# Unsplit multiplication of every pair in the message sweep, from twelve load buffers

## The reference

```python
h = relu(layernorm(x))
msg = adj.T @ h                          # message sweep
x = x + msg * (1 / adj.sum(axis=0))[:, None]    # an infinite inverse becomes 0
h = relu(layernorm(x))
x1 = swish((adj @ h) @ W + b)            # second sweep, first half
x2 = swish((adj @ x1) @ W + b)           # second sweep, second half
x = x + x2
```

## Time and profile before

| | us |
|---|---|
| runs | 684.11, 687.60, 690.33 |
| median | 687.6 |
| profiled execution | 688.42 |
| its span | 686.6 |
| TensorE busy | 634.4 (92%) |
| GpSimd busy | 571.2 (83%) |
| VectorE busy | 523.1 (76%) |
| ScalarE busy | 301.4 (44%) |

### The profile page before, as it was taken

One profiled execution on the slowest core, in us unless ns is written; L12 is line 12 of the kernel. 1 busy time (PEld: TensorE's weight loads), 2 busy tenths in 40 slices (PEclk: granted clock), 3 DMA queues, 4 the chain that ended last, 5 costly groups with the idle time before them and its releaser, 6 DMA issues.

```text
span 686.6 us, 6755 instructions
## 1 busy us (share of the span) xinstructions
PE 634.4 (92%) x2212; PEld 404.0 (59%) x2212; DVE 523.1 (76%) x516; ACT 301.4 (44%) x378; POOL 571.2 (83%) x287
## 2 busy tenths in 40 slices
PE   4888978999998988899999999999999999799994
PEld 2355545666665645556666666667666557466553
DVE  3965789979978839777787777878778778577871
ACT  1943243264272343646445445445444434245250
POOL 2288488689788857998999999999999789599693
PEclk9989999999999998999999999999999999899998
DMA  8999996989999899999999999919999999999941
GB/s 277 352 303 306 298 366 246 329 300 333 329 292 309 286 233 250 345 345 317 328 345 330 329 345 317 279 25 195 327 345 345 315 328 332 305 252 347 311 94 31
DMA packets 155762, 199.80 MB, mean 291 GB/s; under 512 B 5456, under 2 KB 138832, under 8 KB 155728
## 3 DMA queue, kind: packets, MB, share of 16 engines
q1 hardware_dynamic: 86672, 133.18, 62.5%
q10 hardware_dynamic: 69056, 66.20, 35.0%
HBM read 197.26 MB, written 2.10 MB: 290 GB/s over the span
## 4 chain that ended last, share of the span: by engine, by line
PE 55%; POOL 20%; issue 12%; DMA 4%; ACT 3%; DVE 3%; ACTq 1%; SPq 1%; POOLq 0%
PE dg L351 20%; POOL a_lo L701 11%; PE dg L368 9%; PE dg L357 9%; PE dg L358 9%; POOL at_lo L715 7%; PE m_ps L277 4%; DMA raw<-in_adj_dram 2%; PE m_ps L376 2%; DMA h<-in_x_dram 2%; POOL norm L684 1%; PE m_ps L295 1%; PE m_ps L282 1%; PE m_ps L283 1%; ACTq L217 1%
## 5 line engine op out<-in xcount | busy, mean ns | idle before, releaser
L715 POOL TENSOR_TENSOR at_lo<-turned,at_hi 128x1024 fp32r<-128x1024 f32 x160 | 379.8, 2414 | 33.1 <-ACT at_hi L455 28.3
L602 DVE STREAM_TRANSPOSE turned<-raw 128x1024 f32<-128x1024 f32 x256 | 304.1, 1224 | 95.7 <-PE dg L351 41.9
L455 ACT ACTIVATE at_hi<-turned 128x1024 fp32r<-128x1024 f32 x160 | 167.3, 1057 | 208.8 <-DVE turned L602 122.2
L701 POOL TENSOR_TENSOR a_lo<-raw,a_hi 128x1024 fp32r<-128x1024 f32 x66 | 155.1, 2387 | 46.7 <-ACT a_hi L425 44.7
L351 PE MATMUL dg<-turned,f_w 128*128 128x512 f32 x384 | 182.4, 597 | 1.3 <-issue 1.3
L559 DVE TENSOR_TENSOR dg<-raw,dg 128x2048 f32<-128x2048 f32 x60 | 137.5, 2291 | 35.5 <-DMA raw<-in_adj_dram 33.6
L357 PE MATMUL dg<-at_hi,f_hi 128*128 128x512 f32 x320 | 134.9, 422 | 11.5 <-ACT at_hi L455 11.5
L368 PE MATMUL dg<-at_lo,f_hi 128*128 128x512 f32 x320 | 130.9, 490 | 3.1 <-POOL at_lo L715 3.1
L358 PE MATMUL dg<-at_hi,f_lo 128*128 128x512 f32 x320 | 128.4, 401 | 0.0
L277 PE MATMUL m_ps<-raw,h 128*128 128x512 f32 x248 | 116.6, 617 | 11.1 <-DMA raw<-in_adj_dram 11.1
L351 PEld LDWEIGHTS dg<-turned,f_w 128*128 128x128 f32 x384 | 73.2, 191 | 57.0 <-issue 48.5
(11 more groups left out here) (47 smaller groups left out, 258.8 us busy)
## 6 DMA issues: line engine op xcount, KB each, us to landing
raw<-in_adj_dram SPq DMA_DIRECT2D x64, 1024.0 KB, 8.9
raw<-in_adj_dram ACTq DMA_DIRECT2D x122, 512.0 KB, 13.5
raw<-in_adj_dram SPq DMA_DIRECT2D x118, 512.0 KB, 11.7
x<-in_x_dram SPq DMA_DIRECT2D x16, 128.0 KB, 13.5
out_dram<-zs ACTq DMA_DIRECT2D x16, 128.0 KB, 10.9
h<-in_x_dram SPq DMA_DIRECT2D x1, 768.0 KB, 9.3
h<-in_x_dram SPq DMA_DIRECT2D x1, 256.0 KB, 3.3
w<-in_L_gnn_W_dram ACTq DMA_DIRECT2D x1, 64.0 KB, 3.0
```

The costliest lines, as they stand in the source:

```text
L455: act.activation(at_hi[:, s % RING3], turned[:, unit % TURN], ACT.Copy).then_inc(hi3_done, 1)
L602: dve.transpose(dst, src).then_inc(t3_done, 1)
L701: pool.tensor_tensor(a_lo[:, s % RING1], raw1[:, v % RAW1, i], a_hi[:, s % RING1].bitcast(f32), ALU.subtract).then_inc(lo1_done, 1)
L715: pool.tensor_tensor(at_lo[:, s % RING3], turned[:, unit % TURN], at_hi[:, s % RING3].bitcast(f32), ALU.subtract).then_inc(lo3_done, 1)
```

## The change

All 64 pairs are multiplied whole. The rings `a_hi` and `a_lo`, the features `h_hi` and `h_lo`, and everything that fills or awaits them are gone; `raw1` has 12 buffers. A pair's load waits for pair v - 12, added and multiplied. The places in memory of the second sweep are ordered anew: `nT`, `zs` and `at_hi` lie over `raw1` buffers 0 to 3, pieces 1, 2 and 3 over buffers 4 to 9, so that their loads wait for pairs 54, 56 and 58. ScalarE issues its part of pieces 0 to 3 at the head of the last quarter, ahead of `relu2(2)` and the last `copy_message`. The second part of a message's turn moves from behind pair 6 to behind pair 9 of the next quarter, VectorE's add of it from 11 to 12 and its statistics from 12 to 13. GpSimd's scale and remainders of a quarter follow one another with nothing between.

```diff
-RAW1 = 5
-RING1 = 5
+RAW1 = 12
...
-        a_hi = sb("a_hi", [P, RING1, QC], f32r, into=sweep1)
-        a_lo = sb("a_lo", [P, RING1, QC], f32r, into=sweep1)
         h = sb("h", [P, NT, P], into=sweep1)
-        h_hi = sb("h_hi", [P, 2 * len(SPLIT_ROWS), P], f32r, into=sweep1)
-        h_lo = sb("h_lo", [P, 2 * len(SPLIT_ROWS), P], f32r, into=sweep1)
...
+        nT = sb("nT", [P, 2, QC], into=sweep2)
+        zs = sb("zs", [P, 2, QT, P], into=sweep2)
+        at_hi = sb("at_hi", [P, RING3, UC, GROUP], f32r, into=sweep2)
+        spare = sb("spare", [P, 1024], into=sweep2)
         raw3 = {n: sb(f"raw3_{n}", [P, GB, BC], into=sweep2) for n in (1, 2, 3)}
+        at_lo = sb("at_lo", [P, RING3, UC, GROUP], f32r, into=sweep2)
...
             if i in (1, 2, 3):
-                pairs = QUARTERS * PAIRS - (2 if i == 1 else 0)
-                eng.wait_ge(main1_done, pairs)
-                eng.wait_ge(lo1_done, 2 * split_before(pairs))
+
+                pairs = QUARTERS * PAIRS - RAW1 + 2 * i
+                eng.wait_ge(p1_done, pairs)
                 eng.wait_ge(deg_added, pairs)
...
                     sp.wait_ge(deg_added, back + 1)
-                    if whole1(back):
-                        sp.wait_ge(main1_done, back + 1)
-                    else:
-                        sp.wait_ge(lo1_done, 2 * split1(back) + 2)
+                    sp.wait_ge(p1_done, back + 1)
...
+            def p1(v):
                 q, k = v // PAIRS, v % PAIRS
+                pe.wait_ge(raw1_loaded[v % RAW1], 16 * (v // RAW1 + 1))
+                pe.wait_ge(h_ready, 2 * k + 2)
+                for half in range(2):
+                    cols = slice(half * 512, (half + 1) * 512)
+                    if k == 0 and q > 0:
+                        pe.wait_ge(msgT_copied, 2 * (q - 1) + half + 1)
+                    for i in range(2):
+                        mm = pe.matmul(m_ps[:, cols], h[:, 2 * k + i], raw1[:, v % RAW1, i, cols],
+                                       start=k == 0 and i == 0, stop=k == PAIRS - 1 and i == 1)
+                    if half == 0 and k == PAIRS - 1:
+                        mm.then_inc(half_done, 1)
+                mm.then_inc(p1_done, 1)
...
-                if v >= PAIRS and v % PAIRS == 6:
+                if v >= PAIRS and v % PAIRS == 9:
                     turn_message(v // PAIRS - 1, 1)
...
-            for v in splits1:
...
-            relu2(QUARTERS - 2)
-            load3(act, 1, ACT_BLOCKS)
-            copy_message(QUARTERS - 1)
+            for q in range(QUARTERS):
+                if q >= 2:
+                    relu2(q - 2)
+                if q == QUARTERS - 1:
                     load3(act, 0, SP_BLOCKS + ACT_BLOCKS)
+                    for i in range(1, RAW3):
+                        load3(act, i, ACT_BLOCKS)
+                    relu2(q - 1)
+                copy_message(q)
...
-                    if k == 11:
+                    if k == 12:
                         add_message(q, 1)
-                    if k == 12:
+                    if k == 13:
                         node_statistics(q, 1)
...
-            for v in splits1:
...
-            lo_h2(QUARTERS - 2)
+            for q in range(QUARTERS - 1):
+                scale_shift(q * QT, (q + 1) * QT, len(HEAD) + q)
+                lo_h2(q)
```

More of the change, by code:

```diff
@@ L98, in build @@
         f3_w = sb("f3_w", [P, UC * len(WHOLE3), P], into=sweep2)
[L99 to L103, removed]
+        gap = sb("gap", [P, 1536], into=sweep2)
         raw3[0] = sb("raw3_0", [P, GB, BC], into=sweep2)
@@ L145, in build @@
         block = ctx.enter_context(nc.Block())
[L149 to L159, removed]
         def whole3(unit):
@@ L260, in _ @@
         def _(pe):
-            def main1(v, half):
+            def p1(v):
                 q, k = v // PAIRS, v % PAIRS
[L264 to L314, removed]
+                pe.wait_ge(raw1_loaded[v % RAW1], 16 * (v // RAW1 + 1))
@@ L381, in _ @@
             for v in range(QUARTERS * PAIRS):
-                pair1(v)
+                p1(v)
                 if v >= PAIRS and v % PAIRS == 2:
                     turn_message(v // PAIRS - 1, 0)
-                if v >= PAIRS and v % PAIRS == 6:
+                if v >= PAIRS and v % PAIRS == 9:
                     turn_message(v // PAIRS - 1, 1)
@@ L413, in head @@
                 for t in range(*HEAD[b]):
-                    if t // 2 in SPLIT_ROWS:
-                        relu(h_hi[:, 2 * SPLIT_ROWS.index(t // 2) + t % 2], h[:, t], t)
                     relu(h[:, t], h[:, t], t).then_inc(h_ready, 1)
[L418 to L425, removed]
             def copy_message(q):
@@ L449, in hi3 @@
                 if s == 0:
-                    act.wait_ge(main1_done, QUARTERS * PAIRS)
-                    act.wait_ge(rest1_done, len(splits1))
+                    act.wait_ge(p1_done, QUARTERS * PAIRS)
+                    act.wait_ge(deg_added, QUARTERS * PAIRS)
                 if s >= RING3:
@@ L486, in _ @@
                 head(b)
-            for v in splits1:
-                if v >= PAIRS and v == splits1[split_before(v // PAIRS * PAIRS)]:
-                    copy_message(v // PAIRS - 1)
-                hi1(v)
-                if v >= 2 * PAIRS and v == splits1[split_before(v // PAIRS * PAIRS)]:
-                    relu2(v // PAIRS - 2)
-                if v // PAIRS == QUARTERS - 1 and v % PAIRS == 6:
+            for q in range(QUARTERS):
+                if q >= 2:
+                    relu2(q - 2)
+                if q == QUARTERS - 1:
                     load3(act, 0, SP_BLOCKS + ACT_BLOCKS)
-            relu2(QUARTERS - 2)
-            load3(act, 1, ACT_BLOCKS)
-            copy_message(QUARTERS - 1)
+                    for i in range(1, RAW3):
+                        load3(act, i, ACT_BLOCKS)
+                    relu2(q - 1)
+                copy_message(q)
             for unit in range(UNITS3):
@@ L502, in _ @@
                 i = unit // QU + RAW3 - 1
-                if unit in (1, 2):
-                    load3(act, unit + 1, ACT_BLOCKS)
                 if unit % QU == 0 and RAW3 <= i < len(PIECES) and i not in KEPT:
@@ L687, in scale_shift @@
                     .then_inc(norm_ready, 1)
-            def lo_h(k):
-                r = 2 * SPLIT_ROWS.index(k)
-                pool.wait_ge(h_ready, 2 * k + 2)
-                pool.tensor_tensor(h_lo[:, r:r + 2], h[:, 2 * k:2 * k + 2], h_hi[:, r:r + 2].bitcast(f32),
-                                   ALU.subtract).then_inc(h_lo_ready, 1)
-            def lo1(v):
-                for i in range(2):
-                    s = 2 * split1(v) + i
-                    pool.wait_ge(hi1_done, s + 1)
-                    if s >= RING1:
-                        pool.wait_ge(rest1_done, (s - RING1) // 2 + 1)
-                    pool.tensor_tensor(a_lo[:, s % RING1], raw1[:, v % RAW1, i], a_hi[:, s % RING1].bitcast(f32),
-                                       ALU.subtract).then_inc(lo1_done, 1)
             def lo_h2(q):
@@ L728, in _ @@
                 scale_shift(lo, hi, b)
-            for v in splits1:
-                q, k = v // PAIRS, v % PAIRS
-                if q == 0:
-                    lo_h(k)
-                if v == splits1[len(SPLIT_ROWS) - 3]:
-                    for late in SPLIT_ROWS[6:]:
-                        lo_h(late)
-                lo1(v)
-                if q >= 1 and k == 14:
-                    scale_shift((q - 1) * QT, q * QT, len(HEAD) + q - 1)
-                if q >= 2 and k == 3:
-                    lo_h2(q - 2)
-            lo_h2(QUARTERS - 2)
+            for q in range(QUARTERS - 1):
+                scale_shift(q * QT, (q + 1) * QT, len(HEAD) + q)
+                lo_h2(q)
             for unit in range(UNITS3):
```

9 lines of the change are left out of this document (2 added, 7 removed).

## The result

The changed kernel takes 683.4 us (median of 20 runs, 679.66 to 688.97), the kernel before 688.0 (median of 20, 682.87 to 697.07). The ratio is 0.994, with a 95% interval of 0.9911 to 0.9969. So it is faster, by 0.6% or some 4 us; the forecast was 679.3 us, 1.2%. The profiled execution has a span of 682.2 us, 4.4 less than before.

What follows compares the result with a forecast made beforehand. TensorE bounds the second sweep's middle; the message sweep is held by loads and late-released buffers. Span 686.6 - 8.3 (turn) = 678.3, plus 1.8 around it 680.1, less 0.8 for the median: 679.3 us; range 671 to 689.

Steps and rivals of the forecast that it cites:

- the 678.3 of the sum: Whole kernel: forecast span, 686.6 us before less 8.3 us saved in the turn between the sweeps.
- I let it start pair 20 at 86.5: Message sweep: TensorE starts pair 20 at 86.5 us, as 26.35 MB at 307 GB/s land at about 86 us.
- 151.4 + 5.4 + 0.7 = 157.5: Message sweep after pair 20: 44 pairs at 3.44 us, message turns 5.4 us, pipe refilling 0.7 us; end at 244.0.
- The 0.7 us of margin: Message sweep: 0.7 us added for the pipe refilling at the waits of the message turns.
- Rival (a): Message sweep ends at 248, not 244, through waits at quarter ends or the late copy; time 684 us; chance 0.25.
- rival (c): Message sweep: 512 B rows run at line rate, TensorE its own bound from 19.82, end 240.6, time 676 us; chance 0.05.
- The prices: TensorE's work: whole pair 3.44 us, split pair 2.73, so unsplit 0.71 dearer; 33 pairs add 23.4 us.
- Rival (b): Message sweep: loads behind pair 20 run at 307 GB/s, not 380; TensorE ends at 264, time 699 us; chance 0.13.
- The turn: Between the sweeps: GpSimd's fourteenth remainder ends at 283.7 against 292.05 us, through early pieces and relu; 8.3 us saved.
- VectorE's slip: Turn between the sweeps: VectorE has about 18 us of work against GpSimd's 14.3, so 1.1 us is allowed.
- Sweep 2 beyond: Second sweep behind the turn: only memory places change, cost 0 (-2 to +2 us); the 4.40 us stall may recur.
- The order of the queues: Last quarter: ScalarE's relus and load issues finish 5 us or more before the message copy; cost 0, otherwise 3 to 5.

## Why the prediction was right or wrong

**Wrong in size, in the main by one term.** The direction and the mechanism held: work added to TensorE, waits taken away, and the gain in the turn. The span came out 3.9 us over the 678.3 of the sum: 3.2 in the message sweep (247.2 for 244.0), 0.6 less in the turn, and 1.3 more behind it. The term that failed is "I let it start pair 20 at 86.5". TensorE started it at 87.04 + 3.44 = 90.5 us, 4.0 us later. I took the time at which the bytes had been moved (26.35 MB at 307 GB/s) for the time at which TensorE is fed. At 304 GB/s these bytes were moved by 87 us, but pair 20 was not there; the bytes of later loads are among them. VectorE's add of pair 20, which waits for the same load:

```profile
89.12 2.30 DVE L479 TENSOR_TENSOR dg<-raw,dg 128x2048 f32<-128x2048 f32 x1 [1.71 <-DMA raw<-in_adj_dram]
```

Two things were left out. The loads came 4.0 us apart in this stretch, not 3.8, and pair 18 began at 81.33; at 4.0 us a pair, pair 20 would have begun at 89.3 (it landed at 89.1), which is 2.8 of the 4.0. And the first message turn, 2.2 us behind pair 18, falls into a stretch without slack, of which 1.2 us came through; I had counted only the turns behind pair 20. All other terms of the sweep held: 156.7 us from pair 20 to the end against 151.4 + 5.4 + 0.7 = 157.5. The 0.7 us of margin gave back a part, hence 247.2 for 244.0. Some of that is chance, as the same feed gave 245.5 to 248.2 in other runs, but all of these lie above 244. The run with the node loads moved, which has no such stretch, came out at 241.25 by the same prices.

**Rival (a)** gave the end of the message sweep at 248 and a time of 684, and that is nearly what came, but for another reason than it named: quarter ends and the late copy cost nothing (no gap there in the order of time).

**The Trainium skill's rule on 512 B rows, rival (c)** ("DMA: Bandwidth & Descriptors", Specifications). I held it against the trace and rejected it, since the stretch with the node loads ran at 312 GB/s. The rows were right about the time and I was wrong about the reason. With 512 B rows in two rows a partition over all 128 partitions the stretch ran at 395 GB/s, so the row size alone is not what slowed it; the narrow shape, 32 partitions, made 310 (and 64 KB loads of one row a partition 287, for a reason left open). The time that (c) gave for the sweep's end, 240.6, is what came when the destination was wide (240.7).

**The prices.** 0.71 us a pair between whole and split held twice: 3.43 us a pair after, and 8.5 us for 12 pairs. Rival (b), the load as bound behind pair 20, is out: TensorE never waited there, and 383 GB/s was reached. What paid for the 23.4 us of added work is in the stretch from 20 us to the sweep's end, before and after:

```profile
20.00:243.60 223.60, 208.18 (x700) 128.80 (x700) 186.98 (x177) 95.20 (x140) 174.12 (x93) 0.96 0.95 308
20.00:247.20 227.20, 223.75 (x568) 101.37 (x569) 175.68 (x180) 28.54 (x70) 14.99 (x19) 1.00 1.00 329
```

TensorE's idle time fell from 15.4 to 3.5 us, 12.0 in all. With 3.6 us of longer sweep some 8 us are left, and the clock, 0.96 before and 1.00 after, is the likely place; that is an estimate from the difference.

**The turn** was forecast at 283.7 - 244.0 = 39.7 us and measured 39.1, but by two errors that cancel. The fourteen of the earlier trace rows count a remainder that starts at 292.04 and barely falls into the stretch: the one that ends at 292.05 is the thirteenth, 2.4 us too much in my sum. And I allowed 1.1 us for VectorE's slip where the holes were 2.84; I had counted one slow step of its inversion, and there were two (2.33 and 2.29). The reason I gave, the early pieces and the early relu, held, but not as a sum of two: late pieces alone cost 2.4 us, a late scale alone 1.9, and both together 6.1, since the late relu then holds back piece 1.

**Sweep 2 beyond** behaved nearly as said: the stall came again (5.20 us, at 592.34; the earlier trace rows had 4.40), and all behind the turn took 1.3 us more than before, inside the 2 us that I allowed. No run takes this apart. **The order of the queues** in the last quarter was cost at 0, and the copy of the message waited for nothing but TensorE.

## What to carry to other kernels

When an edit takes waits away from an engine that it gives more work, price the work first: here 23 us were added and only some 20 us vanished with it (12 of idle time, the rest most likely of slow clock), and the gain came from a place next door. Where a load's arrival is the bound, take the time from when the consumer starts, not from bytes over rate, and count every other step of the consumer that falls into the same stretch. A ring's depth pays only where something holds its buffers: five did as well as twelve, within the spread of the runs. And once one engine is the bound, hand it the cheaper form of the work as far as idle engines can prepare it: twelve split pairs ended the message sweep 8.5 us sooner, and the time fell by 6.6. When two late things stand in one queue, putting back each alone doesn't price them both.

## What the runs showed of the hardware that was not expected

128 KB loads onto 32 partitions slowed the stream that they stood in far more than their bytes: 310 GB/s with them, 395 GB/s when the same rows went to 128 partitions, two to each, both with 512 B rows and the DMA share full (1.05 and 1.04). A share near 1 therefore didn't mean that the stream was at its best rate. And widening was not enough by itself: 64 KB loads of one row to each of 128 partitions gave 287 GB/s at a share of 0.86.

A step of VectorE over 128x8 elements took 0.17 us before GpSimd's remainders began, and 2.33 and 2.29 us beside them, about as long as one remainder (2.38). And a late start of the chain of GpSimd's work cost less than half of its lateness (1.9 of 4.9 us), as the holes further on closed.
